# Attention with a fused router: the rank products of the second router and the slots made from them, one unit of heads later

## Chip, cores and metric

One core of a Trainium2 chip. The time is that of the device in microseconds (us), the median of several executions; less is better. The engines are called as in the profile: PE is TensorE (PEld its weight loads), DVE is VectorE, ACT is ScalarE, POOL is GpSimd, SP is SyncE.

## What is computed

Two layers on 16 sequences of 256 tokens by 512 channels. The change lies in the second layer, whose reference reads, cut to what matters:

```python
# x: [16, 256, 512] after the first layer
x = x + tanh(g_xattn[1]) * causal_attention(layernorm(x), ctx, ctx)   # 16 heads of 32
x = x + tanh(g_ffn[1]) * moe(layernorm(x))

def moe(x):                          # E = 64 experts, K = 6, CAP = 64, per sequence of T = 256
    scores = softmax(x @ gate_w.T)
    topk_w, topk_i = top_k(scores, K)
    pos = rank of each (token, k) among all pairs with the same expert
    slot = where(pos < CAP, pos, CAP)            # pairs past the capacity are dropped
    buf[topk_i, slot] = x[token]
    y = (silu(buf @ w_gate) * (buf @ w_up)) @ w_down            # per expert
    out = sum over k of y[topk_i, slot] * topk_w * (pos < CAP)
    return out + (silu(x @ sw_gate) * (x @ sw_up)) @ sw_down     # shared expert
```

## The kernel before

The kernel runs phases one after the other: setup, the first layer's recurrence with its router, the first layer's experts, then `attention_phase`, and `routed1_phase`, which streams the expert weights of the second layer. The change lies in `attention_phase` alone, which stands between about 940 and 1850 us of the profiled span.

That phase makes one *turn* per sequence (`b`, 16 of them). The first, second, third and last turns are written out, the others run in a loop of two turns per round. A turn walks through eight *units* `u` (two heads each). Each engine has its own program with its own `turn(b)`, and the order of the work on an engine is exactly the order in which these functions issue it; the engines are tied together by semaphores only. In one unit:

- PE (`turn` in the tensor block): `transpose(b, u)`, six transposes of the exponentials (L1419), which wait for ACT's `exps`; `scores(b, u + 1)` (L1406, with the causal mask L1409), in unit 7 those of the next turn's unit 0; then `back` (L1442) in even units; in unit 5 (`PRE_AT`) `pre`, the transposes of the next sequence's queries (L1376), which need both transpose banks empty; in unit 0 `down(·, 1)` of the sequence before last; then `behind(b.before(), u)`; then `values(b, u // 2)` (L1433) in odd units. Behind unit 7 stands `down(b.before(), 0)`, with `back` inside it.
- DVE: `probs(b, u)` empties one transpose bank (L1725), `maxima(b, u + 1)` makes the row maxima of the next unit's scores (L1720), for which ACT's `exps` (L1567) wait; then one step of the router; then `hidden`; then `outputs` in even units. At the end of unit 7 the next turn's `maxima(·, 0)`, then `outputs(b, 3)` and `residual`.

The feed-forward part of the sequence before, the shared expert and the router, is woven into the units of the current one. On PE this is `behind`: `logits` in unit 1, `logits_back` in unit 2, `gate_up(n)` (products of the shared expert's gate and up matrices, L328) in the units 1 to 6 with n = u - 1, and `ranks`. `ranks` (L1476) waits for `chosen_s` and issues five bf16 products of 64 columns, which count for each token and expert how many earlier pairs chose that expert. On DVE the router's steps are `logit_max` in unit 2, `route` in unit 3, `choose` in unit 4 (ends in the reduction to `chosen`, L1775, which ranks reads) and `slots` in unit 5. `slots` (L1782 to L1800) waits for `rank_s`, turns the ranks into list positions and pairs in eleven instructions with waits between them, and signals `pair_s`. `hidden(n)` (L1807 to L1812) makes the shared expert's hidden values from ACT's tanh, in the units 2 to 6 with n = u - 2, and `hidden(5)` in unit 7; `gate_up(n)` waits for `hidden(n - 2)`, and `down(·, 0)` for `hidden(5)`.

POOL's `scatter` (L1678) writes the pairs into the list in HBM by indirect DMAs, two in each unit of the turn after the one in which `slots` ran. `logits` of the next sequence waits for `pair_s` too. SP loads the next sequence and stores finished rows; its loads wait for merges, scores and values of turns before.

For the last sequence the router has no attention to stand behind: `behind(LAST, u)` runs on PE after all turns, with the ranks at `u == 3`, and DVE calls the same steps in a row.

Of the kernel before, what the change touches and what calls it, by code (L numbers as in the profile page):

```python
# [1183 lines left out]
def attention_phase(nc, io, c):  # L1184
# [3 lines left out]
    with Memory(nc, "attn_") as m:  # L1188
# [73 lines left out]
        with nc.Block() as block:  # L1262
# [107 lines left out]
            def _(pe):  # L1370
# [74 lines left out]
                def logits(b):  # L1445

                    pe.wait_ge(freed, 2 + FB1 * b.i + TJ)
                    wait(pe, pair_s, b.i)
                    for k in range(KC):
                        for z in range(2):  # L1450
                            ins = nc.tensor.matmul(route_ps[z * E1:(z + 1) * E1, 0:T], wr[:, k, :], xnT[z][:, k, :].bitcast(F32),
                                                   start=(k == 0), stop=(k == KC - 1))
                    ins.then_inc(lgT_s, 1)

                def logits_back(b):

                    pe.wait_ge(lgT_ev, b.i + 1)
                    for j in range(TJ):
                        ins = nc.tensor.matmul(route_ps[:, j * E1:(j + 1) * E1], lgT[:, j * P:(j + 1) * P], fold[:], start=True, stop=True)
                    ins.then_inc(logit_s, 1)  # L1460

                def gate_up(b, n):
                    pe.wait_ge(freed, FB1 * b.i + TJ + n + 1)

                    for col, at0 in ((0, n * P), (T, WHOLE + n * P)) if n < M1 - 1 else ((0, 2 * WHOLE),):
                        for k in range(KC):
                            ins = product(nc, ffn_ps[n % 2][:, col:col + T], [w[:, k, at0:at0 + P] for w in wgu],
                                          [x[:, k, :] for x in xnT], k == 0, k == KC - 1)
                    ins.then_inc(gu_s, 1)

                def ranks(b):

                    pe.wait_ge(chosen_s, b.i + 1)
                    for r, parts in enumerate((((c.before, 0),), ((c.before, 1), (c.ones, 0)), ((c.ones, 0), (c.ones, 1)))):
                        for n, (lhs, j) in enumerate(parts):
                            ins = nc.tensor.matmul(route_ps[:, (RANK + r) * E1:(RANK + r + 1) * E1], lhs[:], chosen[:, j, :],  # L1476
                                                   start=(n == 0), stop=(n == len(parts) - 1))
                    ins.then_inc(rank_s, 1)
# [10 lines left out]
                def behind(b, u):  # L1489

                    if u == 1:
                        if b.first:
                            pe.wait_ge(weights_in, 16)
                            pe.wait_ge(high_s, PARTS)
                            pe.wait_ge(low_s, PARTS)
                        logits(b)
                    if u == 1 and b.first:
                        pe.wait_ge(init_s, 3)
                    if u == 2:
                        logits_back(b)  # L1500
                    if 0 < u <= M1:
                        gate_up(b, u - 1)
                    if u == (3 if b.last else 4):
                        ranks(b)

                def turn(b):
# [32 lines left out]
                for u in range(UNITS):  # L1539
                    behind(LAST, u)  # L1540
# [167 lines left out]
            def _(dve):  # L1708
# [3 lines left out]
                def norm_pre(b):  # L1712
                    dve.wait_ge(merged, K0 * (b.i + 1))
                    norm1.dve(nc, dve, b, x[b.s])

                def maxima(b, u):
                    dve.wait_ge(score_s, UNITS * b.i + u + 1)
                    score_ps = banks_of(b, u)
                    for j in range(TJ):
                        v.tensor_reduce(nmax[u % 2][:, :, j], score_ps[:, :, KEYS[j]],  # L1720
                                        AX.X, ALU.max, negate=True).then_inc(max_s, 1)

                def probs(b, u):
                    dve.wait_ge(tr_s[0], use(b, u) + 1)
                    v.tensor_copy(prT[u % 4][:, 0].rearrange("p k t -> p (k t)"), tr_ps[0][:, 0:3 * P]).then_inc(tr_ev[0], 1)  # L1725
# [18 lines left out]
                def logit_max(b):  # L1744
                    dve.wait_ge(logit_s, b.i + 1)
                    v.tensor_reduce(nlmax[:], route_ps[:, 0:TJ * E1].rearrange("p (j e) -> p j e", j=TJ), AX.X, ALU.max,
                                    negate=True).then_inc(nlmax_s, 1)
# [18 lines left out]
                def choose(b):  # L1766

                    posts.need(posts.n)
                    for j in range(TJ):
                        n = posts.did(v.tensor_tensor(hot[:, j], c.expert_no[:].unsqueeze(1).to_broadcast([P, K1, E1]),  # L1770
                                                      self_[:, j, :].unsqueeze(2).to_broadcast([P, K1, E1]), ALU.is_equal))
                    posts.need(n)
                    wait(dve, rank_s, b.i)
                    with nc.allow_low_precision(reason="each sum is 0 or 1"):
                        v.tensor_reduce(chosen[:], hot[:].rearrange("p j k e -> p j e k"), AX.X, ALU.add).then_inc(chosen_s, 1)  # L1775
# [26 lines left out]
                def hidden(b, n):  # L1802

                    dve.wait_ge(tg_s, M1 * b.i + n + 1)
                    s, r = n % 2, width(n)
                    up = ffn_ps[s][0:P, T:2 * T] if n < M1 - 1 else ffn_ps[s][r:2 * r, 0:T]
                    posts.need(posts.did(v.scalar_tensor_tensor(sg[s][0:r], tg[s][0:r], 1.0, ffn_ps[s][0:r, 0:T], ALU.add, ALU.mult)))  # L1807
                    posts.need(posts.did(v.tensor_tensor(sg[s][0:r], sg[s][0:r], up, ALU.mult)))
                    if n == 0:
                        wait(dve, down_s, TJ * b.i)  # L1810
                    posts.need(posts.did(v.tensor_copy(hT[0][0:r, n, :], sg[s][0:r])))
                    v.tensor_tensor(hT[1][0:r, n, :], sg[s][0:r], hT[0][0:r, n, :], ALU.subtract).then_inc(freed, 1)  # L1812

                def shared(b, j):
                    dve.wait_ge(down_s, TJ * b.i + j + 1)
                    v.scalar_tensor_tensor(x3[b.s][:, j, :], ffn_ps[j][:], c.gate_half[:, 3:4], x3[b.s][:, j, :],
                                           ALU.mult, ALU.add).then_inc(freed, 1)

                def ffn_inputs(b):
                    posts.turn(b.i)  # L1820
                    for j in range(TJ):
                        dve.wait_ge(xn_high, TJ * b.i + j + 1)
                        v.tensor_tensor(columns(xnT[1], j), blocks(ffn_ps[j]), columns(xnT[0], j), ALU.subtract).then_inc(freed, 1)

                def turn(b):
                    for u in range(UNITS):
                        probs(b, u)
                        if u + 1 + b.first < UNITS:
                            maxima(b, u + 1 + b.first)
                        elif not b.first:  # L1830
                            hidden(b.before(), M1 - 1)
                        if u == 0 and b.third:
                            for j in range(TJ):
                                shared(b.before().before(), j)
                        if u == PRE_AT - 2 and not b.last:
                            norm_pre(b.after())
                        if not b.first:
                            if u == 0:
                                ffn_inputs(b.before())
                            elif u == 2:  # L1840
                                logit_max(b.before())
                            elif u == 3:
                                route(b.before())
                            elif u == 4:
                                choose(b.before())
                            elif u == 5:
                                slots(b.before())
                            if 1 < u < M1 + 1:
                                hidden(b.before(), u - 2)
                        if u == UNITS - 1 and not b.last:  # L1850
                            maxima(b.after(), 0)
                        if u and u % 2 == 0:
                            outputs(b, u // 2 - 1)
                    outputs(b, GROUPS - 1)
                    residual(b)
# [459 lines left out]
```

## Time and profile before

| | |
|---|---|
| median of 3 runs | 2268.88 us (2267.6 to 2269.99) |
| the profiled execution | 2263.69 us, its span 2261.9 us |
| mean granted TensorE clock | 0.949 |
| PE busy | 1961.1 us, 87% of the span |
| DVE busy | 1298.7 us, 57% |
| ACT, POOL busy | 758.5 us (34%), 870.8 us (38%) |

The busy shares are averages over all phases. A timeline row gives start, duration, engine, line of the kernel, operation and operands; the square bracket, where there is one, is the idle time of that engine before the instruction and what ended it. An instruction without a bracket followed the one before it on its engine. The granted clock is a share of full speed: 1.00 is TensorE at 2.4 GHz, 0.50 at 1.2 GHz. Names of buffers that share memory appear under one name (`second_ffn_room`).

### The profile page before, as it was taken

The page shows a single profiled execution, that of the slowest core. Times are in us where ns is not written, and L with a number is a line of the kernel's source. Part 1 is how long each engine was busy: PE and PEld are TensorE (multiplying, and loading weights), DVE is VectorE, ACT ScalarE, POOL GpSimd, SP SyncE. Part 2 cuts the span into 40 slices and gives each one's busy share as a digit, 9 for nine tenths or more (in the row PEclk, how much of TensorE's full clock was granted, in tenths as well). Part 3 has the DMA queues.
Part 4 walks back from the last instruction along what each step waited for, and adds up shares of the span by engine and source line. Part 5 has one row for each costly group of instructions (what it writes and reads, how often), then busy time and mean ns, then how long its engine had stood idle before and what let it go on. Part 6 is the DMA issues. An engine that isn't in the chain of part 4 may idle for free. (4 is left out here: it accounts for less than half of the span.)

```text
span 2261.9 us, 38805 instructions
## 1 busy us (share of the span) xinstructions
PE 1961.1 (87%) x11898; PEld 1397.6 (62%) x11899; DVE 1298.7 (57%) x3013; ACT 758.5 (34%) x2192; POOL 870.8 (38%) x840
## 2 busy tenths in 40 slices
PE   1988888986999999569999999999999959888886
PEld 1666666664777777347777777777777754433332
DVE  5888888884644444236777777676767632222221
ACT  2333233222422222254555455454554401111110
POOL 5556555543633434152333333333333241212211
PEclk9999999998999999659999999999999989999998
DMA  6432222223333333331111111111111239999996
GB/s 214 162 94 74 87 90 84 84 79 99 104 103 98 100 103 104 125 107 66 67 67 67 66 67 66 67 66 67 66 67 66 100 133 410 409 400 406 406 400 208
DMA packets 113561, 319.48 MB, mean 141 GB/s; under 512 B 31298, under 2 KB 39490, under 8 KB 105220
## 3 DMA queue, kind: packets, MB, share of 16 engines
q1 hardware_dynamic: 86388, 264.83, 31.2%
q0 software_dynamic: 26880, 52.68, 8.1%
q8 instruction: 88, 1.44, 0.3%
q14 instruction: 61, 0.50, 0.1%
q10 hardware_dynamic: 144, 0.03, 0.0%
HBM read 257.33 MB, written 62.33 MB: 141 GB/s over the span
## 5 line engine op out<-in xcount | busy, mean ns | idle before, releaser
L1567 ACT ACTIVATE attn_pr<-attn_score_ps,attn_nmax 128x128 f32<-128x128 f32 x496 | 201.9, 419 | 201.4 <-DVE attn_nmax L1720 201.4
L1678 POOL DMA_INDIRECT list<-attn_pair,attn_pos x192 | 192.0, 1000 | 72.3 <-issue 61.1
L328 PE MATMUL attn_ffn_ps<-attn_xnT_high,attn_wgu_high 128*128 128x256 f32 x704 | 208.9, 297 | 9.1 <-DVE attn_hT_low L1812 8.2
L328 PE MATMUL attn_ffn_ps<-attn_xnT_low,attn_wgu_high 128*128 128x256 f32 x704 | 200.4, 285 | 0.0
L328 PE MATMUL attn_ffn_ps<-attn_xnT_high,attn_wgu_low 128*128 128x256 f32 x704 | 200.3, 284 | 0.0
L300 POOL TENSOR_SCALAR attn_norm_var_eps<-attn_norm_mean_var 128x2 f32<-128x2 f32 x32 | 7.9, 248 | 469.6 <-DVE attn_norm_mean_var L294 469.5
L527 PE MATMUL wkv_ffn_ps<-wkv_xnT,wkv_wg 128*128 128x256 f32 x512 | 146.7, 437 | 25.3 <-DVE wkv_x L842 24.2
L1965 POOL DMA_INDIRECT out<-routed_ym,routed_place x32 | 50.2, 1569 | 300.5 <-DMA out<-routed_ym,routed_place 275.1
L1720 DVE TENSOR_REDUCE attn_nmax<-attn_score_ps 128x2 f32<-128x256 f32 x248 | 126.2, 551 | 62.2 <-PE attn_score_ps L1409 61.2
L328 PEld LDWEIGHTS attn_ffn_ps<-attn_xnT_high,attn_wgu_high 128*128 128x128 f32 x704 | 136.0, 193 | 19.7 <-DVE attn_hT_low L1812 13.1
L1011 POOL DMA_INDIRECT y<-routed_ys,first_ffn_pair x72 | 73.5, 1021 | 183.6 <-DVE routed_ys L1161 179.4
L527 PEld LDWEIGHTS wkv_ffn_ps<-wkv_xnT,wkv_wg 128*128 128x128 f32 x512 | 107.3, 218 | 50.5 <-DVE wkv_x L842 31.3
L328 PEld LDWEIGHTS attn_ffn_ps<-attn_xnT_low,attn_wgu_high 128*128 128x128 f32 x704 | 136.1, 193 | 0.0
L328 PEld LDWEIGHTS attn_ffn_ps<-attn_xnT_high,attn_wgu_low 128*128 128x128 f32 x704 | 136.0, 193 | 0.0
L1419 PE MATMUL attn_tr_ps<-ident,attn_pr 128*128 128x128 f32 x768 | 115.5, 289 | 21.5 <-ACT attn_pr L1567 21.3
L328 PE MATMUL routed_gu_ps<-routed_wgu_high,routed_xT_high 128*128 x288 | 120.1, 417 | 4.5 <-POOL first_ffn_wgu_low L968 4.5
L527 PE MATMUL wkv_ffn_ps<-wkv_xnT,wkv_wu 128*128 128x256 f32 x512 | 122.3, 382 | 0.0
L1725 DVE COPY second_ffn_room<-attn_tr_ps 128x384 f32<-128x384 f32 x96 | 52.9, 551 | 118.6 <-PE attn_tr_ps L1419 92.1
L1406 PE MATMUL attn_score_ps<-second_ffn_room 32*128 32x256 f32 x992 | 118.7, 358 | 0.7 <-issue 0.7
L328 PE MATMUL routed_gu_ps<-first_ffn_wgu_low,routed_xT_high 128*128 x288 | 113.8, 395 | 0.0
L328 PE MATMUL routed_gu_ps<-routed_wgu_high,routed_xT_low 128*128 x288 | 113.3, 393 | 0.0
L1419 PEld LDWEIGHTS attn_tr_ps<-ident,attn_pr 128*128 128x128 f32 x768 | 87.3, 146 | 41.3 <-issue 32.9
(286 smaller groups left out, 4792.9 us busy)
## 6 DMA issues: line engine op xcount, KB each, us to landing
second_ffn_room<-in_w_gu SPq DMA_DIRECT2D x16, 2816.0 KB, 37.9
routed_wgu<-in_w_gu SPq DMA_DIRECT2D x16, 2816.0 KB, 38.2
second_ffn_room<-in_w_down SPq DMA_DIRECT2D x16, 1536.0 KB, 31.3
routed_wdn<-in_w_down SPq DMA_DIRECT2D x16, 1536.0 KB, 31.2
wkv_x<-in_x SPq DMA_DIRECT2D x32, 512.0 KB, 4.0
second_ffn_room<-y SPq DMA_DIRECT2D x32, 512.0 KB, 5.4
wkv_vT<-in_ctxT SPq DMA_DIRECT2D x16, 512.0 KB, 4.2
xn<-wkv_xn SPq DMA_DIRECT2D x16, 512.0 KB, 2.8
```

The lines of the kernel that those rows point to most:

```text
L300: nc.gpsimd.tensor_scalar(self.var[:], self.mv[:, :, 1], EPS, None, ALU.add).then_inc(self.rstd_s, 1)
L328: ins = nc.tensor.matmul(out, a[i], b[j], start=start and n == 0, stop=stop and n == 2)
L527: ins = nc.tensor.matmul(ffn_ps[n % 2][:, col:col + T], w[:, k, n * P:(n + 1) * P], xnT[:, k, :], start=(k == 0), stop=(k == KC - 1))
L1011: nc.gpsimd.indirect_dma_start(io["y0"], bass.IndirectOffsetOnAxis(ap=pair[t.s][:, 1:2].bitcast(U32), axis=0), ys[t.s % SLOTS0][:], None, ...
L1406: nc.tensor.matmul(score_ps[:, a, KEYS[j]], qT[b.s][r:r + D, k, j * P:(j + 1) * P], kT[b.s][r:r + D, k, 0:(j + 1) * P], start=(j == 1), st ...
L1419: ins = nc.tensor.transpose(tr_ps[bank][:, col * P:(col + 1) * P], pr[u % 2][:, z // 3, z % 3, :], c.ident[:])
L1567: nc.scalar.activation(pr[u % 2][:, a, j:2 * j + 1, :].rearrange("p k t -> p (k t)"), score_ps[:, a, KEYS[j]], ACT.Exp, bias=nmax[u % 2][: ...
L1678: nc.gpsimd.indirect_dma_start(io["list1"], bass.IndirectOffsetOnAxis(ap=pos[b.s][:, j, k:k + 1], axis=0), pair[b.s][:, j, k, :], None, bo ...
L1720: v.tensor_reduce(nmax[u % 2][:, :, j], score_ps[:, :, KEYS[j]], AX.X, ALU.max, negate=True).then_inc(max_s, 1)
L1725: v.tensor_copy(prT[u % 4][:, 0].rearrange("p k t -> p (k t)"), tr_ps[0][:, 0:3 * P]).then_inc(tr_ev[0], 1)
L1965: nc.gpsimd.indirect_dma_start(io["out"], bass.IndirectOffsetOnAxis(ap=place[q.s % SLOTS1][:].bitcast(U32), axis=0), ym[q.s % SLOTS1][:], ...
```

## The change

On PE, `ranks` of the sequence before moves from unit 4, behind `gate_up(3)`, to unit 5, behind `gate_up(4)`; there `values(b, 2)` follows it. On DVE, `slots` moves from unit 5, where it stood between `maxima(b, 6)` and `hidden(3)`, to unit 6, between `maxima(b, 7)` and `hidden(4)`. What the steps compute, what they wait for and what waits for them by semaphore stays. The last sequence's router keeps its places.

```diff
                     if 0 < u <= M1:
                         gate_up(b, u - 1)
-                    if u == (3 if b.last else 4):
+                    if u == (3 if b.last else 5):
                         ranks(b)
...
                             elif u == 4:
                                 choose(b.before())
-                            elif u == 5:
+                            elif u == 6:
                                 slots(b.before())
                             if 1 < u < M1 + 1:
                                 hidden(b.before(), u - 2)
```

## Rows read from the trace of the kernel before

**Rows 1.** A turn's stretch: us; busy (count) of PE, PEld, DVE, ACT, POOL; PEclk; DMA

```profile
1108.00:1161.00 53.00, 50.12 (x414) 40.34 (x412) 37.58 (x95) 27.48 (x98) 19.67 (x22) 1.00 0.20 71
```

**Rows 2.** Waits of the attention phase: waiting line, releaser, us, times, longest

```profile
PE attn_route_ps L1476 <- DVE attn_chosen L1775: 10.6, 15, 0.7
```

**Rows 3.** One line's instructions: count, ns min/median/max, first and last start

```profile
L1782 DVE SCALAR_TENSOR_TENSOR attn_slot<-attn_route_ps,base x16: 277/277/292, 1042.3 to 1827.9; 128x128 f32<-128x128 f32 x16
```

**Rows 4.** Timeline of DVE, units 4 to 7: start, us, line, operation [idle before]

```profile
1248.64 1.50 DVE L1775 TENSOR_REDUCE attn_chosen<-attn_hot 128x128 bf16<-128x768 f32 x1
...
1252.20 0.55 DVE L1725 COPY second_ffn_room<-attn_tr_ps 128x384 f32<-128x384 f32 x1
...
1253.60 0.28 DVE L1782 SCALAR_TENSOR_TENSOR attn_slot<-attn_route_ps,base 128x128 f32<-128x128 f32 x1
...
1256.92 0.42 DVE L1807 SCALAR_TENSOR_TENSOR attn_silu_gate<-attn_tanh_gate,attn_ffn_ps 128x256 f32<-128x256 f32 x1
...
1259.57 1.02 DVE L1720 TENSOR_REDUCE attn_nmax<-attn_score_ps 128x2 f32<-128x256 f32 x2 [0.52 <-PE attn_score_ps L1409]
...
1260.51 0.41 DVE L1807 SCALAR_TENSOR_TENSOR attn_silu_gate<-attn_tanh_gate,attn_ffn_ps 128x256 f32<-128x256 f32 x1
...
1263.06 0.56 DVE L1725 COPY attn_prT<-attn_tr_ps 128x384 f32<-128x384 f32 x1 [0.32 <-PE attn_tr_ps L1419]
...
1263.53 0.40 DVE L1807 SCALAR_TENSOR_TENSOR attn_silu_gate<-attn_tanh_gate,attn_ffn_ps 64x256 f32<-64x256 f32 x1
...
1265.20 1.02 DVE L1720 TENSOR_REDUCE attn_nmax<-attn_score_ps 128x2 f32<-128x256 f32 x2
```

**Rows 5.** Timeline of PE in the same stretch

```profile
1250.20 0.23 PE L1476 MATMUL attn_route_ps<-attn_chosen,before 128*128 128x64 bf16 x2 [0.72 <-DVE attn_chosen L1775]
...
1250.39 0.87 PE L1419 MATMUL attn_tr_ps<-ident,attn_pr 128*128 128x128 f32 x6
...
1252.80 1.09 PE L1376 MATMUL attn_tr_ps<-ident,second_ffn_room 128*128 128x128 f32 x8 [0.36 <-DVE second_ffn_room L1725]
...
1259.14 0.39 PE L1409 MATMUL attn_score_ps<-causal,ident 128*128 128x256 bf16 x2
...
1262.48 0.87 PE L1419 MATMUL attn_tr_ps<-ident,attn_pr 128*128 128x128 f32 x6 [1.29 <-ACT attn_pr L1567]
...
1264.45 0.41 PE L1433 MATMUL attn_out_ps<-second_ffn_room 128*32 128x256 f32 x2
...
1265.24 0.50 PE L328 MATMUL attn_ffn_ps<-attn_wd_high,attn_hT_high 128*128 128x512 f32 x1
...
1270.01 0.87 PE L1419 MATMUL attn_tr_ps<-ident,attn_pr 128*128 128x128 f32 x6
```

**Rows 6.** Timeline of turn 15 (the last), units 6 and 7, PE and DVE

```profile
1790.20 0.39 PE L1409 MATMUL attn_score_ps<-causal,ident 128*128 128x256 bf16 x2
...
1791.52 1.01 DVE L1720 TENSOR_REDUCE attn_nmax<-attn_score_ps 128x2 f32<-128x256 f32 x2
...
1794.34 0.87 PE L1419 MATMUL attn_tr_ps<-ident,attn_pr 128*128 128x128 f32 x6 [1.45 <-ACT attn_pr L1567]
...
1795.83 0.54 PE L1433 MATMUL attn_out_ps<-second_ffn_room 128*32 128x256 f32 x2 [0.62 <-DVE attn_prT L1725]
```

**Rows 7.** Timeline of POOL at the next turn's start

```profile
1273.08 1.07 POOL L1678 DMA_INDIRECT list<-attn_pair,attn_pos  x1 [0.56 <-issue]
```

**Rows 8.** Timeline of PE in two other turns' starts

```profile
1223.93 1.31 PE L1388 MATMUL attn_ffn_ps<-ident,attn_xn 128*128 128x128 f32 x8 [1.04 <-DVE attn_x L1816]
...
1438.03 1.97 PE L1388 MATMUL attn_ffn_ps<-ident,attn_xn 128*128 128x128 f32 x8 [2.48 <-DVE attn_x L1816]
...
1439.79 1.41 PE L1419 MATMUL attn_tr_ps<-ident,attn_pr 128*128 128x128 f32 x6
```

**Rows 9.** Stretches of 1 us, columns as in rows 1

```profile
1438.00:1439.00 1.00, 0.97 (x5) 0.97 (x6) 0.63 (x1) 1.00 (x6) 0.96 (x1) 0.50 0.10 37
...
1796.00:1797.00 1.00, 1.00 (x16) 0.54 (x8) 0.93 (x4) 0.00 (x0) 0.00 (x0) 0.50 0.00 0
```

## The prediction

> **What bounds the kernel now.** I looked first at the stretches of single turns: in one turn of 53.00 us PE is busy 50.12 us and DVE 37.58 us, at a granted clock of 1.00 [rows 1]. So in the attention phase PE has some 3 us free per turn and DVE some 15, and an average says nothing on whose delay counts at a given place. The waits of PE name one that the change addresses: the rank products of the second router waited 10.6 us in 15 turns for DVE's `chosen` [rows 2]. The list by line says that `slots` runs 16 times, 15 of them inside turns 1 to 15 and the last one behind them, where the change leaves it alone [rows 3]. Then I followed one turn through in order of time, DVE [rows 4] and PE [rows 5], marking for each instruction whether it came at once behind the one before it or after an idle time. A turn has two stretches:
>
> From the `chosen` reduction (1248.64) DVE runs without an idle time up to the evacuation of unit 5's transposes (1252.20) [rows 4]. PE waits for it twice: 0.72 us before the rank products and 0.36 us before the next batch's query transposes (L1376) at 1252.80, which need the bank that DVE empties [rows 5]. DVE sets the time here.
>
> From 1252.80 PE sets it: query transposes, gate_up(4), values(2), transposes and scores of the units 6 and 7. DVE waits 0.52 us for the scores of unit 7, runs maxima(7) at 1259.57, hidden(4) and outputs(2) from 1260.51, waits 0.32 us for the transposes of unit 7, runs probs(7) at 1263.06 and hidden(5) at 1263.53, and is through at 1265.20 [rows 4]. PE, which had waited 1.29 us for unit 7's exponentials at 1262.48, starts down(0) at 1265.24, directly behind hidden(5), and goes on to the next turn's transposes at 1270.01 with no wait noted [rows 5]. DVE's end of hidden(5) is thus what the turn's end hangs on, and DVE has only that 0.32 us of room between maxima(7) and it.
>
> **The change part by part.** *Ranks taken out of unit 4.* PE loses the wait of 0.72 us there, 10.6 us over the turns [rows 2, 5]. But the L1376 transposes after it waited for DVE anyway, and DVE's chain up to 1252.20 (reduction, hidden(2), outputs(1), probs(5)) does not contain the ranks. PE arrives earlier and waits the same amount longer. Gain: 0, at most 10.6 us if DVE were not the one.
>
> *Ranks put behind gate_up(4) in unit 5.* `chosen` is ready at 1250.14 (1248.64 + 1.50), long before PE gets there, so no wait. The five products take the time from the first of them to the next transposes, 1250.39 - 1250.20 = 0.19 us [rows 5], now on the stretch that PE sets. Behind them in PE's queue stand values(2), the transposes of unit 6 and the scores of unit 7; maxima(7) moves from 1259.57 to 1259.76. Bounds: 0 to 0.19 us.
>
> *Slots taken out of unit 5.* From the first instruction at 1253.60 to hidden(3) at 1256.92 it takes 3.32 us [rows 4]. hidden(3) and probs(6) come earlier by at most that, but PE's next dependence on DVE, maxima(7), waited 0.52 us for PE and not the reverse. Gain: 0. In turn 15 it is otherwise: maxima(7) at 1791.52 follows with no idle time, though PE had begun the last products of these scores at 1790.20; with the offset of the usual turn (1259.14 to 1259.57, 0.43 us) and the 0.19 us it could start at 1790.82, 0.70 us earlier [rows 4 to 6].
>
> *Slots put into unit 6, behind maxima(7).* Its 3.32 us now stand ahead of hidden(4), outputs(2), probs(7) and hidden(5) in DVE's queue. Step by step: maxima(7) 1259.76 to 1260.70; slots to 1264.02; hidden(4) and outputs(2), 1260.51 to 1263.06 less the idle 0.32, so 2.23 us, to 1266.25; probs(7) without a wait and hidden(5), 1263.06 to 1265.20 or 2.14 us, to 1268.39. Before it was 1265.20: 0.19 + 3.32 - 0.32 = 3.19 us later. For this wait queue up on PE values(3) (which needs probs(7)) and down(0) (which needs hidden(5)); behind down(0) stand the next turn's transposes, which had no wait and so no room. On DVE, the next maxima move by as much. Nothing else in the order of a turn gives it back, since both chains of the next turn start from here.
>
> *What reads the slots.* The step issues no DMA itself. POOL's scatters of these positions start one turn later, at 1273.08 for the turn before, behind a norm that itself waits for DVE [rows 7]; with slots done by 1264.02 in one turn and read in the next, they cost 0. SP's loads follow scores and maxima and shift with the turn; they are not waited for here, cost 0.
>
> *The sum without the clock.* 14 turns by 3.19 are 44.7 us, turn 15 is 0.89 less, since maxima(7) starts 0.70 us earlier there and not 0.19 us later, so 2.3 us; together 47.0 us.
>
> *The clock.* The new wait of PE at values(3): PE is free at 1264.45 + 0.19 = 1264.64, probs(7) is done at 1266.72 (1263.53 + 3.19), so 2.1 us idle, after 1.29 us a little earlier and before another wait for hidden(5). In the trace an idle time of 1.04 us left eight transposes at 1.31 us, while one of 2.48 us was followed by a clock of 0.50, the level of 1.2 GHz, eight transposes of 1.97 us and six of 1.41 us instead of 0.87 us [rows 5, 8, 9]: 0.66 + 0.54 = 1.20 us lost. In turn 15 two waits of PE of 1.45 and 0.62 us were enough for 0.50 at 1796 [rows 6, 9]; the single 1.29 us of the usual turn is not (clock 1.00) [rows 1, 5]. The new gaps (1.29, 2.1 and the one before down(0)) are together nearer to the cases that fell. Bounds: no turn, 0 us; all 15, 18.0 us. I take 7 turns, because part of the slow stretch would fall on work that waits for DVE anyway: 8.4 us.
>
> The Trainium skill, "TensorE: Matmul & The Clock Gate", section "Why this matters for your kernels", says that idle gaps between bursts of matmuls send TensorE back to half rate; section "HAM oscillation — how this bites in real kernels" shows a loop that pays it in every round. [...]
>
> Sum: 47.0 + 8.4 = 55.4 us. The profiled execution took 2263.69 us (span 2261.9 us and 1.8 us around it), so 2319.1 us by its own time; the median of the runs is 5.2 us higher, 2268.88, which gives 2324.3 us.
>
> **The rivals.** *The wait removed was on the path: faster.* If PE's 0.72 us before the ranks set the time, 10.6 us come back: 2258.3 us. For it: PE is busy 50 of 53 us and this is a wait of it. Against: 0.36 us of waiting for DVE follow directly, and DVE shows no idle time from 1248.64 to 1252.20. It decides if probs(5) starts earlier than today relative to the `chosen` reduction; chance 0.04.
>
> *The slots are hidden: the same.* If DVE had 3.5 us free between maxima(7) and down(0), or if PE had such a wait after down(0) in the next turn, nothing would be lost: 2269 us. For it: DVE is idle 15 us per turn. Against: 0.32 us of it lie in that place, and down(0) to the next transposes has none. Chance 0.04; that half is recovered (some 24 us, 2292 us) 0.06.
>
> *The delay alone, clock untouched.* 47.0 us: 2315.9 us. For it: single gaps up to 1.29 us leave the clock alone. Against: turn 15. Chance 0.26.
>
> *The clock falls in every turn.* 47.0 + 18.0: 2333.9 us. For it: the gaps add up to more than turn 15's. Against: the low stretch may fall on the waits themselves. Chance 0.20.
>
> That the change does nothing is not possible here: both engines' orders are written out, and 15 turns take the new places.
>
> **How the numbers follow.** The forecast has 0.40, the two neighbours on either side, with no drops of the clock and with 15, 0.46 together. These three are all slower, 0.86 with the half-recovered case 0.92. The range, 2308 to 2338 us, takes the two neighbours with some 8 us below the one (a shift of 2.6 instead of 3.19 us per turn) and 4 us above the other, and leaves out the three small cases. Within 0.2% is about what a measurement of this kernel can tell from no change: faster 0.04, same 0.04, slower 0.92.
>
> **What would show it.** In the changed kernel: no wait of PE before the ranks, and a longer one before L1376; probs(5) no earlier; slots between maxima(7) and hidden(4) with 3.3 us; a wait of PE of about 2 us before the values of unit 7 named after probs(7), then one before down(0) named after hidden(5); turns longer by 3.2 us, or by a good 4 us where a granted clock under 1.00 follows the gap. I would be wrong if a turn is not longer by about 3 us (then down(0) was not held by hidden(5)), if maxima(7) starts sooner after probs(5) than today's 7.4 us, or if the time after the gap grows by more than 1.2 us per turn.

## Result and the profile after

The changed kernel takes 2337.77 us (median of 4 runs, 2336.72 to 2344.58) against 2268.36 us: a ratio of 1.0311 with an interval of 1.0292 to 1.0330, 69 us slower. The profiled execution has a span of 2335.0 us and a mean granted clock of 0.928 instead of 0.949. By the ratio (2339 us) the time lies just above the range of the prediction, by the medians at its upper end.

DVE in the units 5 to 7 of a turn of the changed kernel; the rows answer to [rows 4]:

```profile
1335.96 0.55 DVE L1725 COPY second_ffn_room<-attn_tr_ps 128x384 f32<-128x384 f32 x1
...
1341.98 0.56 DVE L1725 COPY second_ffn_room<-attn_tr_ps 128x384 f32<-128x384 f32 x1 [2.98 <-PE attn_tr_ps L1419]
1343.49 1.02 DVE L1720 TENSOR_REDUCE attn_nmax<-attn_score_ps 128x2 f32<-128x256 f32 x2 [0.95 <-PE attn_score_ps L1409]
1344.43 0.28 DVE L1782 SCALAR_TENSOR_TENSOR attn_slot<-attn_route_ps,base 128x128 f32<-128x128 f32 x1
...
1347.76 0.42 DVE L1807 SCALAR_TENSOR_TENSOR attn_silu_gate<-attn_tanh_gate,attn_ffn_ps 128x256 f32<-128x256 f32 x1
...
1349.91 0.55 DVE L1725 COPY attn_prT<-attn_tr_ps 128x384 f32<-128x384 f32 x1
...
1352.03 1.02 DVE L1720 TENSOR_REDUCE attn_nmax<-attn_score_ps 128x2 f32<-128x256 f32 x2
```

probs(5) (1335.96) is followed by maxima(6) and hidden(3), and then DVE is idle for 2.98 us before probs(6): the place that slots left is empty. maxima(7) starts 7.53 us after probs(5), where it was 7.37. slots takes 3.33 us (1344.43 to 1347.76) ahead of hidden(4), probs(7) follows at 1349.91 without an idle time, and hidden(5) is through at 1352.03. From the start of maxima(7) that is 8.54 us, where it was 5.63 [rows 4].

PE in the same stretch, in answer to [rows 5]:

```profile
1336.56 1.09 PE L1376 MATMUL attn_tr_ps<-ident,second_ffn_room 128*128 128x128 f32 x8 [1.21 <-DVE second_ffn_room L1725]
...
1340.36 0.23 PE L1476 MATMUL attn_route_ps<-attn_chosen,before 128*128 128x64 bf16 x2
...
1340.61 0.86 PE L1433 MATMUL attn_out_ps<-second_ffn_room 128*32 128x256 f32 x16
...
1346.39 0.87 PE L1419 MATMUL attn_tr_ps<-ident,attn_pr 128*128 128x128 f32 x6 [1.30 <-ACT attn_pr L1567]
...
1350.51 0.41 PE L1433 MATMUL attn_out_ps<-second_ffn_room 128*32 128x256 f32 x2 [2.07 <-DVE attn_prT L1725]
...
1352.06 0.80 PE L328 MATMUL attn_ffn_ps<-attn_wd_high,attn_hT_high 128*128 128x512 f32 x1 [0.43 <-DVE attn_hT_low L1812]
...
1357.88 0.88 PE L1419 MATMUL attn_tr_ps<-ident,attn_pr 128*128 128x128 f32 x6
```

No wait stands before the rank products (1340.36), and the query transposes wait 1.21 us for DVE instead of 0.36: the wait that the change removed is taken over by the next one. The new wait of 2.07 us is before values(3), named after probs(7). down(0) starts at 1352.06, directly behind hidden(5). It then takes 5.82 us to the next turn's transposes, where it took 4.77 [rows 5]. Among the turns 1 to 14 this is one of the mild ones: down(0) takes 5.6 to 7.5 us there, 6.60 on the mean, where it took 4.76 to 4.79. The waits of PE in the attention phase (line, releaser, us, times, longest) name the same three places:

```profile
PE attn_out_ps L1433 <- DVE attn_prT L1725: 32.3, 15, 3.3
...
PE attn_tr_ps L1419 <- ACT attn_pr L1567: 21.2, 17, 1.3
PE attn_tr_ps L1376 <- DVE second_ffn_room L1725: 17.3, 14, 1.4
```

The granted clock over the thirteen turn lengths between the ends of hidden(5) in turn 1 and in turn 14 (us, busy us by engine, clock, DMA), and in steps of 1 us around the new gap; the same thirteen turns of the kernel before below it:

```profile
1060.70:1814.00 753.30, 680.48 (x5321) 540.94 (x5317) 486.32 (x1223) 350.35 (x1235) 254.77 (x286) 0.94 0.19 65
...
1350.00:1351.00 1.00, 0.49 (x12) 0.32 (x16) 0.97 (x3) 0.00 (x0) 0.00 (x0) 0.98 0.00 0
1351.00:1352.00 1.00, 0.63 (x12) 0.17 (x4) 0.93 (x3) 0.33 (x1) 0.00 (x0) 0.50 0.00 0
1353.00:1354.00 1.00, 1.00 (x4) 0.73 (x3) 0.17 (x2) 0.91 (x5) 0.00 (x0) 0.50 0.00 0
1354.00:1355.00 1.00, 1.00 (x6) 0.81 (x5) 0.00 (x0) 0.81 (x5) 0.00 (x0) 0.81 0.05 16
```

```profile
1053.90:1745.90 692.00, 649.42 (x5322) 520.54 (x5317) 485.49 (x1223) 351.65 (x1235) 254.86 (x286) 1.00 0.20 71
```

Behind the gap the clock stands at 0.50 in most of values(3) and in the first part of down(0). It fell around this gap in all 15 turns. In the thirteen turns it is 0.94 on the mean and was 1.00. They take 753.3 us instead of 692.0, so 4.7 us more each.

### The profile page after: what moved, and what is told of

Read it like the earlier page. It is cut to its first block and busy times, and to the rows that moved or that the text cites. A ratio compares the mean times of both kernels' runs of the same rounds, so it can differ in the third digit from the quotient of the medians.

```text
span 2335.0 us, 38805 instructions
## 1 busy us (share of the span) xinstructions
PE 2000.5 (86%) x11898; PEld 1422.7 (61%) x11899; DVE 1299.8 (56%) x3013; ACT 757.2 (32%) x2192; POOL 870.0 (37%) x840
## 5 line engine op out<-in xcount | busy, mean ns | idle before, releaser
L1419 PE MATMUL attn_tr_ps<-ident,attn_pr 128*128 128x128 f32 x768 | 115.0, 288 | 22.5 <-ACT attn_pr L1567 21.2
L1419 PEld LDWEIGHTS attn_tr_ps<-ident,attn_pr 128*128 128x128 f32 x768 | 86.7, 145 | 45.2 <-issue 36.6
```

Of the source, the lines that this page charges most:

```text
L1419: ins = nc.tensor.transpose(tr_ps[bank][:, col * P:(col + 1) * P], pr[u % 2][:, z // 3, z % 3, :], c.ident[:])
```

## Experiments

**Filling the gap.** What part of the loss is the clock, and what part the delay? PE gets something to do in the gap, and nothing else is altered:

```diff
+                        if u == UNITS - 1 and not b.first:
+                            pe.wait_ge(pair_s, b.i)
+                            for _ in range(22):
+                                nc.tensor.matmul(route_ps[:, P:P + 192], c.ident16[:], c.causal[:, 0:192], start=True, stop=True)
                         if u % 2:
                             values(b, u // 2)
```

> The changed kernel, and in unit 7 of the turns 1 to 15 PE issues 22 extra bf16 products of 192 columns into a part of the router's bank that nobody reads any more, between the next turn's scores and values(3), where it otherwise stood idle for 2.1 us; they wait for the end of slots, which is earlier. Nothing of the result changes. Theory: of the 69 us lost, 47 are the 3.2 us by which slots holds up hidden(5), and the other 22 are TensorE's clock at 0.50 after that gap; with the gap filled the clock stays at 1.00 in the turns and the time is 2268 + 47 = 2315 us (2308 to 2322). Rival (the 22 us come from something else behind down(0), such as DVE's longer chain): 2338 us or some us more, with the clock at 1.00.

Measured: 2318.72 us against 2269.91, ratio 1.0213 (1.0157 to 1.0270), 49 us slower. PE at the place of the gap, then the clock over thirteen turns and behind the gap:

```profile
1346.25 1.98 PE L1527 MATMUL attn_route_ps<-causal,ident 128*128 128x192 bf16 x22
1348.48 0.41 PE L1433 MATMUL attn_out_ps<-second_ffn_room 128*32 128x256 f32 x2 [0.25 <-DVE attn_prT L1729]
...
1350.03 0.51 PE L328 MATMUL attn_ffn_ps<-attn_wd_high,attn_hT_high 128*128 128x512 f32 x1 [0.69 <-DVE attn_hT_low L1816]
...
1354.80 0.88 PE L1419 MATMUL attn_tr_ps<-ident,attn_pr 128*128 128x128 f32 x6
```

```profile
1067.00:1805.00 738.00, 680.62 (x5603) 551.09 (x5599) 485.54 (x1223) 350.38 (x1235) 254.88 (x286) 0.99 0.19 66
1349.00:1352.00 3.00, 2.31 (x22) 1.69 (x15) 2.04 (x6) 1.31 (x6) 0.00 (x0) 1.00 0.04 11
```

The 22 products take the gap but for 0.25 us, the clock behind it is 1.00, and down(0) takes its old 4.77 us again (1350.03 to 1354.80; 4.75 to 4.79 in the turns 1 to 14), although DVE is as late as in the changed kernel and PE does more work. 19 of the 69 us are gone. The theory's 2315 us is met; its rival, 2338, is not. The runs of this kernel differ by more than those of the others (2309 to 2334 us), and the clock still falls now and then (0.99), behind other waits of PE of 1.1 to 1.4 us, so the split is good to some 10 us.

**Slots alone.** Ranks back in unit 4, slots in unit 6:

```diff
-                    if u == (3 if b.last else 5):
+                    if u == (3 if b.last else 4):
                         ranks(b)
```

> The changed kernel with the rank products back in unit 4, so that only slots stands a unit later. Theory: the whole loss comes from the place of slots; the ranks cost 0.19 us per turn in unit 5, so this kernel is 0 to 4 us under the changed one: 2333 to 2338 us, with PE's wait of 0.7 us before the ranks back again. Rival (the ranks in unit 5 are part of the cause, since they stand on the stretch that PE sets): clearly less, 2320 us or under.

Measured: 2330.9 us, ratio 1.0256 (1.0226 to 1.0287). PE of that kernel, and the clock over the same thirteen turns:

```profile
1330.98 0.23 PE L1476 MATMUL attn_route_ps<-attn_chosen,before 128*128 128x64 bf16 x2 [0.73 <-DVE attn_chosen L1775]
...
1333.59 1.09 PE L1376 MATMUL attn_tr_ps<-ident,second_ffn_room 128*128 128x128 f32 x8 [0.36 <-DVE second_ffn_room L1725]
...
1347.38 0.64 PE L1433 MATMUL attn_out_ps<-second_ffn_room 128*32 128x256 f32 x2 [2.07 <-DVE attn_prT L1725]
```

```profile
1064.20:1808.90 744.70, 676.39 (x5318) 536.84 (x5317) 485.65 (x1222) 351.42 (x1235) 254.97 (x286) 0.95 0.19 66
```

The wait of 0.73 us before the ranks is back and the one before the query transposes is 0.36 us again; the gap before values(3) is 2.07 us as in the changed kernel. The time is 7 us under the changed kernel by the medians and 12 by the ratios, more than the 0.19 us per turn of the ranks (2.7 us). The thirteen turns take 744.7 instead of 753.3 us at a clock of 0.95 instead of 0.94, so some of the difference is clock: down(0) takes 6.39 us on the mean here and 6.60 in the changed kernel. And in the changed kernel PE's one long wait before the query transposes is followed by slow transposes in two turns, at 1043.8 and at 1217.8 (1.94 and 1.96 us instead of 1.09); here the clock never fell at that place:

```profile
1217.80 1.96 PE L1376 MATMUL attn_tr_ps<-ident,second_ffn_room 128*128 128x128 f32 x8 [1.21 <-DVE second_ffn_room L1725]
```

What the ranks' place costs in all stays open. Slots alone brings 51 to 65 of the 69 us.

**Half of slots.** On the kernel before, only the last six instructions of slots go to unit 6:

```diff
                             elif u == 5:
-                                slots(b.before())
+                                picked = slots(b.before())
+                            elif u == 6:
+                                slots_rest(b.before(), picked)
...
                         n = posts.did(v.tensor_tensor(pick[:, j], hot[:, j], slot[:, j, :].unsqueeze(1).to_broadcast([P, K1, E1]), ALU.mult))
+                    return n
+
+                def slots_rest(b, n):
                     numbered = posts.did(v.tensor_copy(pair[b.s][:, :, :, 0], tok[:].unsqueeze(2).to_broadcast([P, TJ, K1])))
```

> The kernel before (ranks in unit 4, slots in unit 5), but the last six instructions of slots, from the copy of the token numbers on (1255.50 to 1256.92, 1.42 us), stand in unit 6 behind maxima(7). Theory: probs(7) and hidden(5) move by 1.42 - 0.32 = 1.10 us per turn, 16 us: 2284 us if the clock stays at 1.00, and up to 2306 us if it falls after PE's now shorter gap as it does in the changed kernel. Rival (only the whole step in that place hurts, half of it is hidden in DVE's idle time): 2268 us.

Measured: 2280.79 us, ratio 1.0049 (1.0031 to 1.0067), so 11 us slower (7 to 15), near the 2284 us of the theory. The thirteen turns take 704.5 us instead of 692.0, 1.0 us more each. PE in unit 7:

```profile
1377.70 0.87 PE L1419 MATMUL attn_tr_ps<-ident,attn_pr 128*128 128x128 f32 x6 [1.29 <-ACT attn_pr L1567]
...
1379.91 0.41 PE L1433 MATMUL attn_out_ps<-second_ffn_room 128*32 128x256 f32 x2 [0.16 <-DVE attn_prT L1725]
...
1381.46 0.51 PE L328 MATMUL attn_ffn_ps<-attn_wd_high,attn_hT_high 128*128 128x512 f32 x1 [0.69 <-DVE attn_hT_low L1815]
```

The gaps are 1.29, 0.16 and 0.69 us, and from 1055 to 1770 us the mean granted clock is 0.99. A part of the step costs what exceeds DVE's 0.32 us of idle time: 1.10 us per turn were expected and 1.0 measured. With the shorter gap before values(3) hardly any price of the clock is paid; down(0) ran slowly in three of the turns 1 to 14.

**Ranks alone.** Ranks in unit 5, slots stays in unit 5 but behind hidden(3); the edit is against the changed kernel:

```diff
                             elif u == 4:
                                 choose(b.before())
-                            elif u == 6:
-                                slots(b.before())
                             if 1 < u < M1 + 1:
                                 hidden(b.before(), u - 2)
+                            if u == 5:
+                                slots(b.before())
```

> The rank products in unit 5 as in the changed kernel, but slots stays in unit 5, behind hidden(3) instead of ahead of it. Theory: slots now waits for the ranks behind gate_up(4), until about 1256.95 on the clock of the kernel before, ends at 1260.3, probs(6) follows, maxima(7) starts at 1260.8 instead of 1259.57: 1.2 us per turn, 18 us, 2286 us; and up to 22 us more where the clock falls, since PE's wait before unit 7's transposes grows from 1.3 to 2.5 us. Rival (the ranks' move saves PE its wait of 0.7 us, and slots behind hidden(3) fits into DVE's idle time): 2258 to 2268 us.

Measured: 2312.04 us, ratio 1.0178 (1.0154 to 1.0202), 42 us slower: about what the 18 us of delay and the full price of the clock (22 us) come to, though no run splits the two here. The wait of PE and the clock over the thirteen turns:

```profile
PE attn_tr_ps L1419 <- ACT attn_pr L1567: 37.2, 17, 2.4
```

```profile
1058.60:1794.90 736.30, 676.54 (x5333) 537.29 (x5325) 485.94 (x1224) 348.82 (x1235) 254.49 (x286) 0.96 0.19 67
```

PE's wait for the exponentials of unit 7 has grown from 21.3 us in 17 times to 37.2, up to 2.4 us at once, and the clock is 0.96. At this place in unit 5 the slots do not fit either: once the ranks stand behind gate_up(4), the slots that need them come too late there as well.

**Slots behind hidden(5).** The changed kernel, with slots taken off the way to down(0):

```diff
                         elif not b.first:
                             hidden(b.before(), M1 - 1)
+                            slots(b.before())
...
-                            elif u == 6:
-                                slots(b.before())
```

> The changed kernel, but slots stands in unit 7 behind hidden(5), ahead of the next turn's maxima(0), so that values(3) and down(0) no longer wait for it. Theory (the loss is the delay of hidden(5)): down(0) starts as in the kernel before, PE has no gap at values(3); the next maxima come 3.3 us later, the transposes of the next turn 1.2 us later than PE could take them, and residual 3.3 us later, which hits the five turns behind the loop's jump in full, where PE already waits for DVE: 9 x 1.2 + 5 x 3.3 = 27 us, 2296 us (2285 to 2306). Rival (a step of 3.3 us costs the same wherever it stands behind unit 5, because DVE is full there): 2330 to 2338 us.

Measured: 2319.50 us, ratio 1.0224 (1.0205 to 1.0243), 51 us slower; neither theory's number. PE's waits for the exponentials, then PE in one turn behind the loop's jump and at the start of a usual turn, and the clock over about thirteen turns:

```profile
PE attn_tr_ps L1419 <- ACT attn_pr L1567: 37.3, 29, 1.4
```

```profile
1340.89 0.88 PE L1419 MATMUL attn_tr_ps<-ident,attn_pr 128*128 128x128 f32 x6
...
1349.87 1.48 PE L1388 MATMUL attn_ffn_ps<-ident,attn_xn 128*128 128x128 f32 x8 [2.02 <-DVE attn_x L1816]
1351.14 1.49 PE L1419 MATMUL attn_tr_ps<-ident,attn_pr 128*128 128x128 f32 x6
...
1456.31 1.21 PE L1419 MATMUL attn_tr_ps<-ident,attn_pr 128*128 128x128 f32 x6 [1.37 <-ACT attn_pr L1567]
```

```profile
1060.00:1800.00 740.00, 683.62 (x5328) 545.28 (x5326) 490.25 (x1230) 350.73 (x1238) 254.63 (x286) 0.95 0.19 66
```

The gap at values(3) is gone, but the delay has moved to the next turn. In twelve turns PE now waits 1.24 to 1.37 us before the next turn's first transposes, as I had expected (1.2 us); the waits of L1419 have grown from 21.3 us in 17 times to 37.3 in 29. The five turns behind the loop's jump, which I had expected to pay in full, do not: the transposes of the normed rows wait 2.02 us for DVE in one of them and 0.26 us in the others. What follows such a wait often runs slowly (1.48 and 1.49 us instead of 1.31 and 0.87 [rows 8, 5]): the clock fell 15 times in thirteen turns, where it fell once in the kernel before, and is 0.95 on the mean. My 27 us counted the delays and left the clock out again. Whether it is the clock that makes the other 24 us was not tried by filling this gap.

**Two versions that the waits point to.** On the kernel before, first the norm's statistics of the next sequence in unit 1 instead of unit 3, to take work out of the stretch that DVE sets; then the shared expert's small block first, to cover PE's wait of 1.29 us before unit 7's transposes; then both.

```diff
-                        if u == PRE_AT - 2 and not b.last:
+                        if u == (PRE_AT - 2 if b.first else 1) and not b.last:
                             norm_pre(b.after())
```

```diff
+            def block_of(n):
+                return (n - 1) % M1
...
                 def gate_up(b, n):
                     pe.wait_ge(freed, FB1 * b.i + TJ + n + 1)
-                    for col, at0 in ((0, n * P), (T, WHOLE + n * P)) if n < M1 - 1 else ((0, 2 * WHOLE),):
+                    m = block_of(n)
+                    for col, at0 in ((0, m * P), (T, WHOLE + m * P)) if m < M1 - 1 else ((0, 2 * WHOLE),):
...
                 def hidden(b, n):
                     dve.wait_ge(tg_s, M1 * b.i + n + 1)
-                    s, r = n % 2, width(n)
+                    m = block_of(n)
+                    s, r = n % 2, width(m)
...
-                    v.tensor_tensor(hT[1][0:r, n, :], sg[s][0:r], hT[0][0:r, n, :], ALU.subtract).then_inc(freed, 1)
+                    v.tensor_tensor(hT[1][0:r, m, :], sg[s][0:r], hT[0][0:r, m, :], ALU.subtract).then_inc(freed, 1)
```

> The kernel before with one other step moved: the statistics of the next sequence's norm (1.5 us on DVE) stand in unit 1 instead of unit 3 in all turns but the first. Theory: DVE sets the time from unit 3 to the query transposes of unit 5, PE's waits there (0.72 us before the ranks, 0.36 us before L1376) are both DVE's lateness, and in unit 1 DVE has 5 us of idle time; both waits go, 1.08 us in 14 turns, 15 us: 2254 us. Rival (PE's wait before the ranks has room behind it, or the norm's early place waits for POOL's merge and holds up unit 2): 2268 us or slower.

> The kernel before with the shared expert's blocks in another order: the small block of 64 channels (12 products) comes first, in unit 1, and a full one (24 products) last, in unit 6. Theory: PE's wait of 1.29 us before unit 7's transposes is a wait for the exponentials that PE has too little work to cover; 12 more products take 1.4 us there and 1.4 us less in unit 1: up to 1.29 us in 15 turns, 19 us: 2250 us. Rival (unit 1 then runs into DVE or ACT, or hidden(5) gets its tanh too late): 2262 to 2275 us.

> The norm's statistics in unit 1 and the small block first together, on the kernel before. Theory: the two waits are apart from each other, one in the units 4 and 5, one in unit 7, so the gains add: 2268 - 15 - 19 = 2234 us. Rival (taking one wait away moves it to the other place): no more than the better of the two alone, about 2250 us.

Measured: the norm early 2256.93 us, ratio 0.9949 (0.9933 to 0.9965); the small block first 2245.04 us, 0.9889 (0.9866 to 0.9911); both 2231.43 us, 0.9842 (0.9826 to 0.9859), against 2268.27 us. DVE in the units 1 to 5 with the norm early, then PE's wait for unit 7's exponentials with the small block first:

```profile
1237.19 1.29 DVE L290 BATCH_NORM_STATS2 attn_norm_stats<-second_ffn_room 128x6 f32<-128x512 f32 x2 [2.89 <-POOL second_ffn_room L1662]
...
1250.82 0.55 DVE L1725 COPY second_ffn_room<-attn_tr_ps 128x384 f32<-128x384 f32 x1
1252.01 1.02 DVE L1720 TENSOR_REDUCE attn_nmax<-attn_score_ps 128x2 f32<-128x256 f32 x2 [0.63 <-PE attn_score_ps L1409]
...
1253.99 1.51 DVE L1775 TENSOR_REDUCE attn_chosen<-attn_hot 128x128 bf16<-128x768 f32 x1
...
1257.56 0.55 DVE L1725 COPY second_ffn_room<-attn_tr_ps 128x384 f32<-128x384 f32 x1
```

```profile
PE attn_tr_ps L1423 <- ACT attn_pr L1572: 1.9, 2, 1.2
```

The statistics (1237.19) now run in idle time. DVE had no idle time before maxima(5) and now waits 0.63 us for PE's scores there, so the gain is at most 1.5 less 0.63 us, 0.9 us per turn and not 1.08; the thirteen turns, 683.8 us instead of 692.0, show 0.6. From maxima(5) (1252.01) to probs(5) (1257.56) DVE again runs without a pause, and the two waits of PE that I wanted to remove are still there; the first is down from 10.6 us to 7.5. That the time lies near the theory's 2254 us is thus partly luck. The small block first takes the 21.3 us of PE's wait down to 1.9; its 23 us by the runs (20 to 30) are more than the 19 of the theory, the profiled executions differ by 17.6, and what the rest is stays open. Together the gains add: 11 and 23 us alone, 37 us in one kernel. That version beats both kernels.

## Why the prediction was right and wrong

*Ranks out of unit 4: 0 us.* Right, and shown: the wait moved to the query transposes (0.36 to 1.21 us), and with the ranks put back the kernel is 7 to 12 us faster, not slower.

*Ranks in unit 5: 0.19 us.* The products take 0.25 us on PE (1340.36 to 1340.61), and maxima(7) stands 0.16 us later behind probs(5), 2.4 us over 15 turns. Slots alone differs from the whole change by more than that, and what the ranks' place costs beyond it stays open. One way is shown: PE's wait of 0.72 us did not vanish but joined the 0.36 us before the query transposes, and behind the 1.21 us that came of it the clock fell in two turns.

*Slots on the way to down(0): 3.19 us per turn.* Right: 8.54 - 5.63 + 0.16 = 3.07 us in the turn shown. Filling the gap leaves a loss of 49 us (36 to 61) where the sum without the clock was 47.0, and the part of 1.42 us costs 1.0 us per turn, 11 us by the runs, where 1.10 us per turn were worked out.

*The clock: 8.4 us.* This is the term that failed, in size and not in mechanism. I took 7 turns at 1.20 us. The clock fell in all 15 turns, and it is 0.94 on the mean over the thirteen. By the runs, with 69 us in all and 47 for the delay, it cost 22 us, and the filled kernel gives back 19; over 15 turns that is 1.3 to 1.5 us each. By the trace down(0) alone is longer by 1.83 us on the mean of the turns 1 to 14 (6.60 instead of 4.77), 26 us; 47 and 26 come to the 73 us by which the spans of the two profiled executions differ (2335.0 and 2261.9). Two things were misjudged. I counted only 7 turns because part of the slow stretch would fall on work that waits for DVE anyway. A part did, but 56 of the 89 us at 0.50 around this gap in the turns 1 to 14 fell on down(0), which nothing covers. And I took the price of a fall from fourteen transposes behind another gap, so that even my bound for all 15 turns, 18.0 us, was too low. The rival with the clock falling in every turn, 2333.9 us, which I gave 0.20, was the nearest. The Trainium skill, "TensorE: Matmul & The Clock Gate", section "HAM oscillation — how this bites in real kernels", shows a loop that pays the fall in every round. This kernel did so too, in all 15 turns, but behind shorter idle times (1.30 and 2.07 us) than that section speaks of; by the page alone the count could not have been forecast.

*The rivals.* Neither the faster one nor the hidden one is left: PE's wait before the ranks had room behind it, and DVE's 15 idle us per turn lie elsewhere (2.98 us of it now before probs(6), in front of the place where it was needed). The delay alone is ruled out by the clock of 0.94 and by the filled kernel.

## What to carry to other kernels

A step that is moved on an in-order engine costs what it delays behind its new place, not what it frees at the old one; follow from both places to the next instruction that another engine waits for, and read the idle time of the moved engine up to there (here 0.32 us for a step of 3.3 us). A wait that vanishes is a gain only if the next wait of the same engine is not on the same releaser. And when a change opens gaps on PE in every round of a loop, price the clock over all rounds, and by the work that stands behind the gap in that place.

## What the runs showed of the hardware

No single length of idle time decided whether the granted clock fell; where PE's waits were longer, it fell in more of the turns. Of the turns 1 to 14, down(0) ran in part at 0.50

- in none of the kernel before, where PE's one wait ahead of it is 1.2 to 1.3 us;
- in two with the norm early, where that wait is the same;
- in three with half of slots (1.2 to 1.3 and some 0.2 us);
- in eleven with the ranks alone (2.2 to 2.4 us at once);
- in all fourteen of the changed kernel (1.2 to 1.3 and 2.1 us); in twelve of them the clock fell while PE still stood in the second gap.

A fall behind a single wait of 1.29 us, in the kernel with the norm early:

```profile
1373.10 0.87 PE L1419 MATMUL attn_tr_ps<-ident,attn_pr 128*128 128x128 f32 x6 [1.29 <-ACT attn_pr L1567]
```

```profile
1375.00:1378.00 3.00, 3.00 (x21) 1.77 (x20) 1.86 (x6) 1.25 (x6) 0.00 (x0) 0.50 0.03 5
```

In the gap of 2.07 us, 22 small bf16 products of 192 columns, whose results nobody reads, were enough to keep the clock at 1.00 in down(0) in all those turns: adding work to PE made that kernel 19 us faster.
